# Spreading a layer norm over eight slots, max transposes at the end of their slot, and GpSimd fills ahead of the first power, in a fused mixer, attention and expert kernel

## What is computed

```python
def reference(x, ctx_512, ...):
    # 1. state space mixer on the layer norm of x
    x = x + mixer(_layernorm(x), w_norm, W_in, w_conv, dt_bias, A_log, W_h2i, W_out)
    # 2. cross attention, 32 query heads of 16, 8 key heads, keys and values are ctx_512
    x = x + attention(_layernorm(x), ctx_512, ctx_512)
    # 3. mixture of 16 experts (2 per token) and a shared expert
    x = x + ffn(_layernorm(x), gate_w, expert_bias, shared_*, experts_*)
    return x

def mixer(x, ...):
    xn = x * rsqrt(mean(x * x) + EPS) * w_norm
    z, xi, dt, B, C = split(xn @ W_in.T)
    xi = silu(causal_conv4(xi)); dt = softplus(dt + dt_bias)
    h[t] = exp(dt * A) * h[t-1] + dt * mean(xi per head) * B;  y[t] = sum(h[t] * C)
    return (y @ W_h2i.T * silu(z)) @ W_out.T + residual      # the residual is the layer norm of x

def attention(q, k, v):
    return softmax(q @ k.T / 4) @ v
```

## Time and profile before

| | us |
|---|---|
| median of three runs | 1300.86 |
| the profiled execution | 1302.54 |
| its span (first to last instruction) | 1300.7 |
| TensorE busy | 1224.2 |
| VectorE busy | 684.4 |
| ScalarE busy | 481.4 |
| GpSimd busy | 313.6 |

### The profile page before, as it was taken

The page is one execution under the profiler, slowest core; times in us unless marked ns, Lnnn a source line. Parts: engine busy times, 40 slices in busy tenths (PEclk is TensorE's granted clock), DMA queues, the critical chain, the costliest instruction groups (busy, mean ns, idle before and its releaser), DMA issues. The chain is left out here.

```text
span 1300.7 us, 14817 instructions
## 1 busy us (share of the span) xinstructions
PE 1224.2 (94%) x5045; PEld 508.3 (39%) x5046; DVE 684.4 (53%) x1110; ACT 481.4 (37%) x681; POOL 313.6 (24%) x459
## 2 busy tenths in 40 slices
PE   4989989999999999999999999999978999999996
PEld 2444433333333434333333333333334444444442
DVE  5843585655687465667564766767347222212211
ACT  1311223533554443555353455555510122222221
POOL 3312310221320220221022121111102244333443
PEclk9999999999999999999999999999987999999998
DMA  6320775103274201263400245000029465577641
GB/s 175 100 87 21 184 153 106 31 13 110 68 146 77 66 22 25 82 129 80 100 12 13 94 82 78 34 2 2 33 74 338 103 142 123 154 219 214 177 82 23
DMA packets 113218, 122.71 MB, mean 94 GB/s; under 512 B 19024, under 2 KB 78544, under 8 KB 112896
## 3 DMA queue, kind: packets, MB, share of 16 engines
q1 hardware_dynamic: 102624, 100.76, 29.8%
q0 software_dynamic: 10528, 21.12, 7.9%
HBM read 96.20 MB, written 28.97 MB: 96 GB/s over the span
## 5 line engine op out<-in xcount | busy, mean ns | idle before, releaser
L654 DVE TENSOR_REDUCE mx<-ps_m 128x2 f32<-128x1024 f32 x256 | 313.3, 1224 | 263.1 <-PE ps_m L1087 261.6
L797 ACT ACTIVATE prob<-ps_s 128x1024 f32<-128x1024 f32 x256 | 262.2, 1024 | 380.0 <-PE ps_s L1070 380.0
L1012 PE MATMUL acc<-xnT,wring 128*128 128x512 f32 x560 | 279.7, 599 | 3.5 <-DVE xz L574 1.8
L1708 PE MATMUL ps_gu<-ring,xgT 128*128 x376 | 176.9, 593 | 1.5 <-issue 1.5
L1087 PE MATMUL ps_m<-k_stack,q_stack 96*128 96x512 bf16 x512 | 153.0, 380 | 9.0 <-DVE mx L654 7.3
L1070 PE MATMUL ps_s<-q_stack,k_stack 99*128 99x512 bf16 x512 | 153.8, 382 | 4.4 <-ACT prob L797 4.1
L1442 DVE COPY xgT<-ps_x 128x512 f32<-128x512 f32 x47 | 32.5, 692 | 207.7 <-PE ps_x L1680 203.2
L1100 PE MATMUL ps_o<-prob,values 128*32 128x512 f32 x1024 | 136.4, 605 | 0.0
L1012 PEld LDWEIGHTS acc<-xnT,wring 128*128 128x128 f32 x560 | 102.6, 190 | 69.7 <-issue 34.6
L1402 POOL DMA_INDIRECT out<-y,dest x47 | 74.5, 1585 | 158.8 <-DMA out<-y,dest 115.4
L1070 PEld LDWEIGHTS ps_s<-q_stack,k_stack 99*128 99x128 bf16 x512 | 35.5, 97 | 182.4 <-issue 133.3
(11 more groups left out here) (255 smaller groups left out, 1215.6 us busy)
## 6 DMA issues: line engine op xcount, KB each, us to landing
ring<-in_w_experts SPq DMA_DIRECT2D x96, 256.0 KB
wring<-in_w_in SPq DMA_DIRECT2D x80, 256.0 KB, 3.5
q_stack<-part_rows SPq DMA_DIRECT2D x96, 128.0 KB, 4.8
wring<-in_w_out SPq DMA_DIRECT2D x32, 256.0 KB, 2.7
part_rows<-part SPq DMA_DIRECT2D x20, 384.0 KB, 3.9
xt<-in_x SPq DMA_DIRECT2D x16, 256.0 KB, 4.3
k_stack<-part_rows SPq DMA_DIRECT2D x48, 64.0 KB, 4.0
xn_rows<-xt SPq DMA_DIRECT2D x3, 1024.0 KB, 4.2
```

Source lines behind the costliest of these rows:

```text
L654: nc.vector.tensor_reduce(mx[:, n % G, 2 * u:2 * u + 2], ps_m[:, :, :], AX.X, ALU.max).then_inc(s_max, 1)
L797: nc.scalar.activation(prob[:, slot % PROB, :, :], ps_s[:, :, :], ACT.Exp, scale=SCALE).then_inc(s_exp, 1)
L1012: ins = nc.tensor.matmul(bank(b, n), weights, xnT[:, k, :], start=(k == 0), stop=(k == KD - 1))
L1708: ins = nc.tensor.matmul(ps_gu[p][:, :], xgT[:, p, k * P:(k + 1) * P], weights(own)[:, k * 2 * F:(k + 1) * 2 * F], start=(k == 0), stop=(k ...
```

## The change

- In the head GpSimd does its six fills before it waits for the first variances; the power comes behind them.
- VectorE normalises the first batch into the buffers `state` and `gains` (`first_xn`), not in place, and no longer computes the first residual; ScalarE computes it from `xt`, which is still whole, with `keep` as scale and bias. The load of the next batch's tokens and the first add to `x1` wait for it (`s_kept`). `keep[:, :, 1]` changes its sign for that, in all batches.
- `transpose_max` comes behind both mixer halves, the max scores and the front, ahead of the products; ScalarE's copy to `mT` comes behind its mixer work and ahead of the front.
- VectorE does `silu_z` ahead of `silu_xi`, `gain`, `rest_y` and `low_y`.
- A front starts at r = -6: one statistic a slot in r = -6 to -3, one normalisation a slot in r = -2 to 1. SyncE stores the rows in r = 2.

```diff
--- before.py
+++ after.py
@@ -123,6 +123,7 @@
+        first_xn = [state[:, 0, :], state[:, 1, :], gains[:, 0, :], gains[:, 1, :]]
         gated = [first_z[:, 0, :], first_z[:, 1, :]] + [xz[:, i, :] for i in range(2, KI)]
@@ -168,6 +169,7 @@
         s_nega = sem("neg_a_ready")
+        s_keep, s_kept = sem("residual_scales"), sem("first_residual")
         s_ve, s_rs, s_ln = sem("variance_ready"), sem("rstd_ready"), sem("hn_ready")
@@ -205,7 +207,7 @@
             at = slot - FRONT
-            return [(a, at - WINDOW * a) for a in range(B - 1) if -4 <= at - WINDOW * a < WINDOW]
+            return [(a, at - WINDOW * a) for a in range(B - 1) if -6 <= at - WINDOW * a < WINDOW]
@@ -337,6 +339,8 @@
                         sp.wait_ge(s_tr, TB * (b + 1))
+                        if b == 0:
+                            sp.wait_ge(s_kept, TB)
                         load_x(b + 1)
@@ -367,7 +371,7 @@
                 for a, r in fronting(slot):
-                    if r:
+                    if r != 2:
                         continue
@@ -454,7 +458,6 @@
             steps.then(nc.gpsimd.memset(half[:, :, :], -0.5))
-            deviations(0)
             nc.gpsimd.memset(head_mean[:, :, :], 0.0).then_inc(s_pad, 1)
@@ -466,6 +469,7 @@
             pool.wait_ge(s_ones, 1)
+            deviations(0)
             for g in range(G):
@@ -551,13 +555,19 @@
                 nc.vector.tensor_scalar(keep[:, :, 0], rstd[:, :, 0], 1.0, None, ALU.add)
-                steps.then(nc.vector.tensor_tensor(keep[:, :, 1], mv[:, :, 0], rstd[:, :, 0], ALU.mult))
+                steps.then(nc.vector.scalar_tensor_tensor(out=keep[:, :, 1], in0=mv[:, :, 0], scalar=-1.0,
+                                                          in1=rstd[:, :, 0], op0=ALU.mult, op1=ALU.mult))
...
                 nc.vector.tensor_scalar(x1[:, b * TB + j, :], xt[:, j, :], keep[:, j, 0:1], keep[:, j, 1:2],
-                                        ALU.mult, ALU.subtract)
+                                        ALU.mult, ALU.add)
                 nc.vector.tensor_scalar(xt[:, j, :], xt[:, j, :], mv[:, j, 0:1], rstd[:, j, 1:2],
+                                        ALU.subtract, ALU.mult).then_inc(s_ln, 1)
+
+            def normalise_first(j):
+
+                nc.vector.tensor_scalar(first_xn[j], xt[:, j, :], mv[:, j, 0:1], rstd[:, j, 1:2],
                                         ALU.subtract, ALU.mult).then_inc(s_ln, 1)
@@ -611,6 +621,8 @@
                 dve.wait_ge(s_out, TB * b + j + 1)
+                if b == 0:
+                    dve.wait_ge(s_kept, TB)
                 slot = x1[:, b * TB + j, :]
@@ -655,26 +667,25 @@
                 tiles = x1[:, TB * a:TB * a + TB, :]
-                if r in (-4, -3):
-                    if r == -4:
+                if -6 <= r < -2:
+                    if r == -6:
                         dve.wait_ge(s_res, G * (a + 1))
-                    for j in (0, 1) if r == -4 else (2, 3):
-                        nc.vector.bn_stats(st[:, j, :], tiles[:, j, :]).then_inc(s_v, 1)
-                        steps.n += 1
+                    nc.vector.bn_stats(st[:, r + 6, :], tiles[:, r + 6, :]).then_inc(s_v, 1)
+                    steps.n += 1
                 if r == -3:
...
                     nc.vector.tensor_scalar(var_eps[:, :, 0], mv[:, :, 1], LN_EPS, None, ALU.add).then_inc(s_fve, 1)
-                if r in (-2, -1):
+                if -2 <= r < 2:
                     if r == -2:
...
                             dve.wait_ge(s_fst, 16 * a)
-                    for j in (0, 1) if r == -2 else (2, 3):
-                        nc.vector.tensor_scalar(xt[:, j, :], tiles[:, j, :], mv[:, j, 0:1], rstd[:, j, 0:1],
-                                                ALU.subtract, ALU.mult).then_inc(s_fn, 1)
+                    j = r + 2
+                    nc.vector.tensor_scalar(xt[:, j, :], tiles[:, j, :], mv[:, j, 0:1], rstd[:, j, 0:1],
+                                            ALU.subtract, ALU.mult).then_inc(s_fn, 1)
                 for i in heavy(a, r):
@@ -705,9 +716,12 @@
             variances(0)
+            dve.wait_ge(s_rs, 1)
+            for j in range(TB):
+                normalise_first(j)
             inverse(0)
-            for j in range(TB):
-                residual(0, j)
+            dve.wait_ge(s_v, steps.n)
+            nc.vector.engine_nop().then_inc(s_keep, 1)
             for j in range(TB):
@@ -733,6 +747,8 @@
                         taps(b, (m - 12) // 2)
+                    if m >= 29 and m % 2 == 1 and (m - 29) // 2 < 7:
+                        silu_z(b, (m - 29) // 2)
                     if m >= 15 and m % 2 == 1 and (m - 15) // 2 < KI:
@@ -744,8 +760,6 @@
                         low_y(b)
-                    if m >= 29 and m % 2 == 1 and (m - 29) // 2 < 7:
-                        silu_z(b, (m - 29) // 2)
                     if m == 42:
@@ -817,6 +831,10 @@
             nc.scalar.activation(neg_a[:, :], neg_a[:, :], ACT.Copy, scale=-1.0).then_inc(s_nega, 1)
+            act.wait_ge(s_keep, 1)
+            for j in range(TB):
+                nc.scalar.activation(x1[:, j, :], xt[:, j, :], ACT.Identity, bias=keep[:, j, 1:2], scale=keep[:, j, 0:1]
+                                     ).then_inc(s_kept, 1)
@@ -828,11 +846,6 @@
                         high_part(5 * e + c + 1)
-                if u == 5 and 0 <= n + 1 < N:
-                    act.wait_ge(s_mtr, n + 2)
-                    if n >= 0:
-                        act.wait_ge(s_mrow, 48 * (n + 1))
-                    nc.scalar.activation(mT[:, :], ps_tb, ACT.Copy).then_inc(s_mev, 1)
                 if u == 2 and 0 <= n - 1 < N:
@@ -905,6 +918,11 @@
                                          ).then_inc(s_icopy, 1)
+                if u == 5 and 0 <= n + 1 < N:
+                    act.wait_ge(s_mtr, n + 2)
+                    if n >= 0:
+                        act.wait_ge(s_mrow, 48 * (n + 1))
+                    nc.scalar.activation(mT[:, :], ps_tb, ACT.Copy).then_inc(s_mev, 1)
                 for a, r in fronting(slot):
@@ -972,7 +990,8 @@
                 for k in range(KD):
-                    ins = nc.tensor.transpose(turned[:, k * P:(k + 1) * P], xt[:, j, k * P:(k + 1) * P], ident[:, :])
+                    rows = first_xn[j] if b == 0 else xt[:, j, :]
+                    ins = nc.tensor.transpose(turned[:, k * P:(k + 1) * P], rows[:, k * P:(k + 1) * P], ident[:, :])
                 ins.then_inc(s_tr, 1)
@@ -1174,8 +1193,6 @@
                     transpose_out(n - 1)
-                if u == 5 and 0 <= n + 1 < N:
-                    transpose_max(n + 1)
                 if b < B and m == 32:
@@ -1190,6 +1207,8 @@
                     front(a, r)
+                if u == 5 and 0 <= n + 1 < N:
+                    transpose_max(n + 1)
                 if slot >= 3 and slot % 2 == 1 and (slot - 3) // 2 < 2 * R * G * TB // 2:
```

## The result

The changed kernel takes 1280.55 us (median of 4 runs, 1280.44 to 1283.15), the kernel before 1300.63 (4 runs, 1298.59 to 1301.11): the medians differ by 20.1 us. The ratio from the runs taken together is 0.9858, 95% interval 0.9842 to 0.9873, which is 18.5 us (16.5 to 20.5). The forecast was 1287.3, with a range of 1283.5 to 1292.5. The direction was right, the gain was larger by half, and it lies outside the range. The profiled execution of the changed kernel took 1283.15 us with a span of 1281.3 (before: 1302.54 and 1300.7), so the two traces account for 19.4 us.

The account below looks back on a forecast made before the run. The prediction took TensorE, busy 94% of the span, as the bound, so only its waits count. Terms of 6.3 + 3.6 + 0.9 + 0.1 + 0.6 + 2.4 - 0.3 = 13.6 us gave 1287.3 us, range 1283.5 to 1292.5.

Parts of the forecast that it names:

- Head, 6.3 us: Kernel start: with fills first and residual on ScalarE, the first projection starts at 16.0, not 22.28; 6.3 us kept.
- That holds by 0.5 us: Second batch's convolution taps: they end at 46.2, before TensorE's weight block needs their bank at 46.7.
- The rival that gave 3.9 us: Second batch's taps: VectorE takes back part of the head, TensorE keeps 3.9 of 6.3; time 1289.7, chance 0.15.
- Fills beside statistics: Head: GpSimd's fills beside VectorE's four statistics do not slow them, about 0.7 us each; no cost taken.
- The rival in which they exclude each other: Head: fills and statistics shut each other out, 3 us less gain; time 1290.3, chance 0.04.
- `ysb`, 3.6, and `mpart`, 0.1: Late max transposes: avoided waits for `ysb` give 1.2 us in each of three batches, for GpSimd's `mpart` 0.1.
- `dtr`, 0.9: Late max transposes: TensorE's three waits for VectorE's `dtr`, 0.9 us together, vanish whole.
- The twelve quiet groups, 0: Groups beside the mixer where the max transposes move and nothing else is late: no gain counted, 0 us.
- Silu, 0.6: Mixer: silu of z ahead of silu of xi shortens TensorE's one 1.22 us wait for `first_z` by 0.6 us.
- Layer norm, 2.4: Layer norm over eight slots: shorter waits for maxima give 0.2 at the first batch, then 1.0 and 1.2 us.
- Rows of the maxima, -0.3: Slot 8 scores: row DMAs issued later delay only the first group, 0.3 us lost.
- the slower rival: Rows of the maxima land after the scores want them in all 32 groups, costing 16 us; time 1303.3, chance 0.03.

Follow-up runs that it names:

- res_only: Changed kernel with GpSimd's fills back behind the first statistics, the first batch's residual still on ScalarE: 1286.36 us, ratio 0.9898.
- t_last: Changed kernel with the max transposes one step later, behind the products and directly ahead of the next slot's scores: 1282.83 us, ratio 0.9856.
- head_old: Changed kernel with both head edits undone, fills behind the statistics and first residual on VectorE: 1284.79 us, ratio 0.9868.
- warm_x: Changed kernel with the second batch's rows requested early and five unused matmuls ahead of the first batch's output step: 1278.67 us, ratio 0.9842.
- control: Changed kernel with only a mask on the expert owner's number, one register operation a tile: 1281.85 us, ratio 0.9861.
- warm_x2: Repetition, beside the changed kernel on one chip, of the changed kernel with early second-batch rows and five unused matmuls: 1278.23 us, ratio 0.9838.
- control2: Repetition of the changed kernel with only the mask on the expert owner's number: 1280.27 us, ratio 0.9854.

## Why the prediction was wrong, step by step

- **Head, 6.3 us.** Right at the first projection (forecast at 16.0, seen at 15.49), too much as a sum at the end, where 3.9 arrive by the medians, give or take 2.5. One step that failed is "That holds by 0.5 us": it took the second batch's variances to be ready at the old time, and they came at 33.72 instead of 32.4 (32.93 and 33.15 in the repetitions), since the rows landed further apart. TensorE then waited 1.79 us in one profile, 2.61 in another and not at all in the third. The rival that gave 3.9 us had this cause, but that its size agrees is luck: the clock, at the start and behind the `csb` wait, was in no case, and how the loss divides between them stays open. By the medians the head makes the forecast too fast by 2.4 us; the miss is in the middle.
- **Fills beside statistics.** Right: 0.69 us each. The rival in which they exclude each other is dead, while `res_only` shows again that normalisations do wait for fills. That is the rule of the Trainium skill, page "SBUF — State Buffer", section "Who interferes with whom", in both halves.
- **`ysb`, 3.6, and `mpart`, 0.1.** Right: three groups of 1.24. The 0.1 has no slot of its own.
- **`dtr`, 0.9.** It measured 2.1: the step "The `dtr` waits, 0.9 us in three, go whole" counted the wait and not the price of the place (0.33 a group, and a little more).
- **The twelve quiet groups, 0.** They gave 4.0 us, and ten groups behind the mixer 0.7 more. This is the step that failed most: the prediction priced the transposes by who waits for them, and let the operation cost the same wherever it stands. The row that tells otherwise was there to be read: L946 spans 0.3 us, and what lies around it could be subtracted in a group without waits, as above.
- **Silu, 0.6.** Mis-sized: 1.0 in the trace (1.4 less 0.4 at m = 44) and by undoing it.
- **Layer norm, 2.4.** 2.7 in the trace, 4.6 by undoing it, since the old form would now also lower the clock at the first batch.
- **Rows of the maxima, -0.3, and the slower rival.** No wait of the scores for row DMAs; this rival is dead and the 0.3 with it.

Middle: 7.3 + 4.0 (quiet) + 0.7 (groups behind the mixer) + 1.2 (`dtr`) + 0.4 (silu) + 0.3 (norm) + 0.3 (rows) - 0.4 (m = 2) + 0.1 (`ysb`) - 0.1 (`mpart`) = 13.8, the measured 13.94 but for hundredths. With 3.9 for the head that is 17.8 of 20.1 by the medians. The kernel before has further medians of 1299.4 to 1300.75 and the changed kernel's lie at 1280.3 to 1281.9, so the distance itself is 18 to 20; up to 2 us are not attributed. Part of them is the next section's.

The range failed because every rival varied how much of the known waits would go, and none asked whether the work that was moved has a price of its own.

## What to carry over

When a short TensorE operation is moved, price it by its place: in a group where nothing waits, subtract the start-to-start distance without it from that with it, at the old and at the new neighbours; multiply by all groups, not by those with waits. A gain at the head of a kernel must be followed through the races and long waits behind it, and with more than one profile: here three profiles of the same code kept 3.4, 6.0 and 4.0 us of it at slot 0. And before a second engine is brought in for a few passes, undo that half alone: here it moved the first projection, and no gain at the end could be measured.

## What the hardware showed beyond that

- **The same code, 7 us apart.** From the first to the last expert matmuls of L1708 (L1727 in the changed kernel) the kernel before takes 272.6 us in its profile; the kernels of the study, with the same code there, 268.5 (`t_last`) to 275.6 (`head_old`, with one wait of 3.1 us for gathered tokens, `xg`). One profile's end says little about 3 us.
- **The clock at the start of the expert phase.** Behind a wait of 7.3 us TensorE's granted clock is 0.50 over 8 us in the kernel before, in the changed one and in `warm_x`, and 0.76 to 0.78 in `control` and `warm_x2`, which are 2.1 us faster there than the changed kernel and `warm_x`. No edit touches this place.
- **Slow matmuls under a clock of 1.00.** In the head the 32 small matmuls of L1020 take 1.94 us in some profiles (the changed kernel, `control`) and 1.08 in others (`control2`, `warm_x`), while the windows' column shows 1.00 for both. In `control2` one sees the change: the head's transposes take 421 ns each up to 14.3 us, and 273 at 14.7. The durations, not that column, tell the level there.
